# Cross-attention scores issued behind the next tile's queries, and the last two feed-forward quads on separate banks and buffers

## The chip, the cores and the metric

One core of one Trainium2 chip runs one program. The metric is the device time of one execution in microseconds (us). Its engines each work through their own list of instructions in order: TensorE (PE, matrix products and transposes into PSUM; PEld is its weight load), VectorE (DVE), ScalarE (ACT), GpSimd (POOL) and SyncE (SP), which issues the DMAs. Semaphores order them: `then_inc` on one instruction, `wait_ge` before another. An engine that waits holds up all that is behind it in its list.

## The reference

The input is `x`, 32 sequences of 64 rows of 128 features, with a context of the same shape. Eight sub-layers are applied one after the other, each to a layer-normalised `x` and added back:

```
x = x + L0_xattn(layernorm(x), ctx)   # 16 heads of 64, full softmax with a mask, own biases
x = x + L0_ffn(layernorm(x))          # 6 layers: local attention (rotary, band mask) + x, then
                                      # layernorm, W1, a * gelu(gate), W2, + x ; tokens shifted
x = x + L1_xattn(...) ; x = x + L1_ffn(...)   # 16 heads of 8 ; an fp8 product
x = x + L2_xattn(...) ; x = x + L2_ffn(...)   # mixture of 8 experts and a shared one
x = x + L3_xattn(...) ; x = x + L3_ffn(...)   # int8-rounded weights ; 8 experts
```

The change touches L0_xattn (the *cross stage*), the end of the six layers of L0_ffn (the *local stage* and its *tail*), and the rounding of L3's weights (`quantise_...`) and L1's fp8 weight, which are done on the side during the cross stage.

## The kernel before

The 2048 rows of `x` are 16 tiles of 128. `layers_tensor`, `layers_scalar`, `layers_vector` and `layers_gpsimd` (one function for each engine) run the same loop over a step number `g`, and the order of the calls in it is the order of the engine's instructions. Steps -16 to -1 start the 16 tiles of the cross stage, one each (`is_cross`). Steps 0 to 95 start the 96 tiles of the local stage (6 layers of 16; `STEPS` is 96). The loop ends at step 109 (`STEPS + OUTPUT`). Then `merged_tensor` and its fellows run L1 to L3.

A tile's work is spread over several steps. In step `g` of the cross stage TensorE does, in this order (letters are used below): the queries of tile g into PSUM `w0` (Q, `cross_queries`, L558), the values of g-1 into `w2` (V, `cross_values`, L578), the keys of g into `w1` (K, `cross_keys`, L568), the output rows of g-3 into `py` (R, `cross_rows`, L597), the transpose of the normalised x of g+1 into `pt` (X, `turn_x`, L551), the transposes of the probabilities of g-2 into `w2` (T, `turn_probs`, L692), the scores of g-1 into `w1` (S, `cross_scores`, 64 small matmuls in `scores_tensor`, L399), and the attention product of g-2 into `w2` (A, `attend_tensor`, L413). VectorE does: `cross_shift` of g-2 (adds the mask, L936, takes the maximum, L429, subtracts it, L432), layer-norm statistics of g+2, the query bias of g (L929), the normalisation of g+2 and of the finished g-4 (L466), the sums of the exponentials of g-2 (L440, L443), the update of x with R (L946), and the output bias of g-2, which copies A's result to `oT` (L956). ScalarE does the exponential of g-2 (L424), then copies V of g-1 (L880), K of g (L883), X of g+1 (`xT`, L855) and T of g-2 (`probT`, L895). GpSimd multiplies the probabilities of g-2 with the reciprocal sums (L454).

The numbers of the instructions are per tile, so `g-2` on VectorE in step g is the tile whose scores TensorE wrote in step g-1. S of g-1 waits for `kT_ready` of g, since it overwrites `w1`; T waits for `prob_ready` of g-2; A for `pT_ready`; V of g-1 for `oT_ready` of g-3; K of g for `masked` of g-2.

In the feed-forward of the local stage four tiles are a *quad*; there are 24. `quad_at(g, lag)` says which quad has its turn: quad Q is transposed into `pt` (`quad_in`, L723) in step 4Q+8, normalised in 4Q+10 (`quad_normalise`, L1022, after `quad_stats` and GpSimd's `quad_rstd`), goes through three hidden chunks (`quad_turn` L729, `affine` L838, `hidden` L741 and L745, `gelu` L844, `gate` L1030) in 4Q+11, and its output (`output`, L752) is added to the rows by `feed` (L1004 to L1007) in 4Q+13. All quads share `pt`, `py`, and the buffers `xs`, `xnT`, `gate` and `hid`. After the last quads `turn_out` (L763, L764) and `add_back` (L1038) bring the rows back to `x`, a quarter at a time, on `w0`, `w1`, `w2`, `w0`.

Of the kernel before, what the change touches and what calls it, by code (L numbers as in the profile page):

```python
# [38 lines left out]
def build(nc, a, out):  # L39
    ctx = ExitStack()  # L40
    with ctx:
# [138 lines left out]
        k.s_k8 = wide(k.straight).rearrange("p (s j n) -> p s j n", s=2, j=8)  # L180
        k.f_int, k.f_mag = (wide(k.sq)[:, i * P:(i + 1) * P].bitcast(mybir.dt.int32) for i in range(2))
# [137 lines left out]
        k.quant.spread = sem("quant_spread")  # L319
        k.quant.done = sem("quant_done")  # L320
# [166 lines left out]
NEWTON = 4  # L487

# [31 lines left out]
def quad_at(g, lag):  # L520

    Q, r = divmod(g - lag, 4)
    return Q if not r and 0 <= Q < ALL_QUADS else None
# [15 lines left out]
def layers_tensor(pe, k):  # L539
    def turn_x(g):  # L540
# [8 lines left out]
        if g - 2 == QUANTISE:  # L549
            pe.wait_ge(k.quant.done, 1)  # L550
# [164 lines left out]
    def quad_in(Q):  # L715

        pe.wait_ge(k.row_added, 2 * Q + 2)
        if Q:
            pe.wait_ge(k.gated, 3 * Q)
        else:  # L720
            pe.wait_ge(k.z_ready, QUADS)
        for j in range(4):
            mm = pe.transpose(k.pt[:, j * P:(j + 1) * P], shifted_rows(k, (4 * Q + j) % TILES), k.ident[:, :])  # L723
        mm.then_inc(k.quad_rows, 1)

    def quad_turn(Q):
        pe.wait_ge(k.quad_norm, Q + 1)
        for j in range(4):
            mm = pe.transpose(k.pt[:, j * P:(j + 1) * P], k.xs[:, 0, j, :], k.ident[:, :])  # L729
        mm.then_inc(k.quad_cols, 1)  # L730

    def hidden(Q, c, g):
        at, n = CHUNKS[c]
        if c == 0:
# [3 lines left out]
            pe.wait_ge(k.z_fed, quads_before(g, OUTPUT))  # L738
        else:
            pe.wait_ge(k.gated, 3 * Q + c)  # L740
        pe.matmul(k.pt[0:n, :], k.c_w1[:, HID + at:HID + at + n], k.xnT[:, :], start=True,  # L741
# [3 lines left out]
        pe.matmul(k.py[0:n, :], k.c_w1[:, at:at + n], k.xnT[:, :], start=True, stop=True).then_inc(k.line_psum, 1)  # L745

    def output(Q, g):
        pe.wait_ge(k.hid_ready, 3 * Q + 3)
        pe.wait_ge(k.row_added, pairs_before(g))
        for c, (at, n) in enumerate(CHUNKS):  # L750
            n += c == 2
            mm = pe.matmul(k.py[:, :], k.c_w2[0:n, c, :], k.hid[0:n, c, :], start=(c == 0), stop=(c == 2))  # L752
        mm.then_inc(k.out_psum, 1)

    def turn_out(q):

# [12 lines left out]
    for g in range(-TILES, STEPS + OUTPUT + 1):  # L769
# [16 lines left out]
        if is_cross(g - 1):  # L786
# [1418 lines left out]
```

## Time and profile before

| | us |
|---|---|
| median of 3 runs | 2528.41 |
| lowest and highest | 2522.78, 2529.38 |
| the profiled execution | 2521.92 |
| its span, first to last instruction | 2520.1 |
| mean granted TensorE clock in it | 0.984 |

The stages lie in the span about as follows: loads and start to 14.6 us, cross stage to about 254, local stage to about 1697, its tail to 1728.4, L1 to L3 to the end. All times below are microseconds from the span's start.

How to read the rows. [...] A row of the timeline has start, duration, engine, line, operation, output<-inputs, form and count, and in brackets how long the engine was idle before it and who released it. The view of one line gives shortest/median/longest duration in ns, and the first and last start in us.

### The profile page before, as it was taken

Reading aid. Unit: us, or ns where it says so; the run is one execution under the profiler, and the core shown is the slowest. Engines: PE = TensorE matmul, PEld = TensorE weight load, DVE = VectorE, ACT = ScalarE, POOL = GpSimd, SP = SyncE. Lnnn points to the kernel's source line nnn. Section 1 sums busy time; section 2 is a strip of 40 time slices with the busy share of each in tenths; the row PEclk is TensorE's granted clock in tenths of the full one; section 3 lists DMA queues with packets and bytes.
Section 4 is the critical chain, followed back from the end, with each engine's and each line's share of the span. In section 5 each row is a group of like instructions: output and inputs, shape, how many; then the busy total and the mean of one; then the engine's idle time right before and its main releaser. Section 6 shows DMA issues by size and latency. Waiting matters only on the chain.

```text
span 2520.1 us, 60784 instructions
## 1 busy us (share of the span) xinstructions
PE 2371.4 (94%) x25500; PEld 1437.9 (57%) x25500; DVE 1904.4 (76%) x3471; ACT 1453.2 (58%) x2047; POOL 1186.5 (47%) x883
## 2 busy tenths in 40 slices
PE   6787899999999999999999999988889999999999
PEld 5666556566665666666665666554555555455443
DVE  4666999999999899999999999965866766455222
ACT  2233566666666666666666666653467677566443
POOL 1222777777677767777767776741211111001000
PEclk9899999999999999999999999999899999999999
DMA  3000000000010000000000000001000101120110
GB/s 123 6 6 8 2 2 2 27 10 13 2 35 2 13 18 18 7 7 27 10 8 7 27 10 11 2 1 75 18 32 15 35 12 40 41 83 20 38 52 28
DMA packets 36164, 56.27 MB, mean 22 GB/s; under 512 B 6380, under 2 KB 20852, under 8 KB 35640
## 3 DMA queue, kind: packets, MB, share of 16 engines
q1 hardware_dynamic: 35896, 52.40, 6.7%
q8 instruction: 205, 3.36, 0.6%
q14 instruction: 63, 0.52, 0.1%
HBM read 51.19 MB, written 1.19 MB: 21 GB/s over the span
## 4 chain that ended last, share of the span: by engine, by line
PE 54%; DVE 28%; ACT 11%; issue 5%; POOL 1%; SPq 0%; DMA 0%; DVEq 0%; ACTq 0%
PE w L1380 9%; PE w L1370 9%; DVE turned L976 4%; DVE norm L983 4%; PE w L643 4%; PE w L624 4%; PE w L634 4%; PE py L658 4%; PE w L413 3%; DVE top L429 3%; DVE straight_odd L971 2%; DVE logit L432 2%; PE w L711 2%; ACT sq L877 2%; PE w L1499 2%
## 5 line engine op out<-in xcount | busy, mean ns | idle before, releaser
L424 ACT ACTIVATE prob<-logit 128x512 f32<-128x512 f32 x224 | 137.5, 630 | 299.0 <-DVE logit L432 299.0
L1370 PE MATMUL w<-qT,m_fc 128*128 128x512 f32 x544 | 267.7, 605 | 0.4 <-ACT turned L1617 0.4
L1122 POOL TENSOR_TENSOR straight_odd<-straight_odd,turned 128x1024 f32<-128x1024 f32 x96 | 227.5, 2370 | 82.5 <-DVE turned L976 79.6
L454 POOL TENSOR_TENSOR prob<-prob,rden 128x1024 f32<-128x1024 f32 x112 | 213.4, 1906 | 99.0 <-DVE rden L443 99.0
L976 DVE TENSOR_TENSOR turned<-w,rot 128x512 f32<-128x512 f32 x384 | 245.3, 680 | 0.0
L1122 POOL TENSOR_TENSOR straight<-straight,turned 128x1024 f32<-128x1024 f32 x96 | 226.6, 2370 | 37.3 <-DVE turned L976 37.3
L1116 POOL TENSOR_TENSOR straight_odd<-straight_odd,rnorms 128x1024 f32<-128x1024 f32 x96 | 180.6, 1903 | 115.3 <-DVE rnorms L997 115.3
L983 DVE TENSOR_REDUCE norm<-sq 128x16 f32<-128x1024 f32 x192 | 224.0, 1207 | 0.0
L1116 POOL TENSOR_TENSOR straight<-straight,rnorms 128x1024 f32<-128x1024 f32 x96 | 180.6, 1901 | 69.9 <-DVE rnorms L997 69.9
L643 PE MATMUL w<-b_wqkv,m_proj 128*128 128x512 f32 x384 | 191.3, 621 | 4.0 <-DVE logit L432 4.0
L890 ACT COPY qT<-w 128x1024 f32<-128x1024 f32 x96 | 97.3, 1014 | 162.0 <-PE w L670 162.0
L624 PE MATMUL w<-b_wqkv,m_proj 128*128 128x512 f32 x384 | 190.4, 618 | 0.0
L634 PE MATMUL w<-b_wqkv,m_proj 128*64 128x512 f32 x768 | 186.0, 605 | 0.0
L473 POOL TENSOR_TENSOR fresh_roots<-fresh_means,eps 128x1 f32<-128x1 f32 x64 | 12.7, 198 | 361.6 <-DVE fresh_means L461 361.6
L658 PE MATMUL py<-oT,b_wo 128*128 128x256 f32 x768 | 175.8, 382 | 1.1 <-ACT oT L911 1.1
L658 PEld LDWEIGHTS py<-oT,b_wo 128*128 128x128 f32 x768 | 147.1, 192 | 42.1 <-issue 22.8
L877 ACT ACTIVATE sq<-w 128x1024 f32<-128x1024 f32 x96 | 98.2, 1023 | 114.2 <-PE w L643 114.2
L692 PE MATMUL w<-ident,prob 128*128 128x128 f32 x896 | 122.0, 281 | 38.1 <-POOL prob L454 37.3
L895 ACT COPY probT<-w 128x1024 f32<-128x1024 f32 x112 | 114.1, 1018 | 75.9 <-PE w L692 75.9
L1617 ACT ACTIVATE turned<-w,m_bfc 128x512 f32<-128x512 f32 x136 | 93.3, 688 | 109.7 <-PE w L1370 106.8
L1617 ACT ACTIVATE straight_odd<-w,m_bfc 128x512 f32<-128x512 f32 x136 | 93.6, 688 | 105.8 <-PE w L1370 103.2
L413 PE MATMUL w<-probT,v 64*64 64x64 f32 x7168 | 134.0, 225 | 21.5 <-ACT probT L895 19.8
(253 smaller groups left out, 5255.5 us busy)
## 6 DMA issues: line engine op xcount, KB each, us to landing
b_wqkv<-gates SPq DMA_DIRECT2D x64, 256.0 KB, 3.7
b_wqkv<-in_b_wqkv SPq DMA_DIRECT2D x18, 512.0 KB, 3.6
ctxT<-in_ctxT SPq DMA_DIRECT2D x64, 64.0 KB, 1.8
b_wo<-in_b_wo SPq DMA_DIRECT2D x6, 512.0 KB, 3.6
m_fc<-in_m_fc SPq DMA_DIRECT2D x1, 2304.0 KB, 9.4
m_proj<-in_m_proj SPq DMA_DIRECT2D x1, 2304.0 KB, 13.0
m_fc<-in_m_fc SPq DMA_DIRECT2D x8, 256.0 KB, 3.5
m_proj<-in_m_proj SPq DMA_DIRECT2D x8, 256.0 KB, 3.4
```

What stands on the lines that cost most here:

```text
L413: mm = pe.matmul(w[64 * c:64 * c + 64, at:at + 64], k.v2[r, s, b, 64 * h:64 * h + 64], k.probT[r, h, 64 * b:64 * b + 64], start=True, stop ...
L454: pool.tensor_tensor(flat, flat, k.rden[:, s, :, None].broadcast_to([P, HEADS, SEQ]), ALU.mult).then_inc(k.prob_ready, 1)
L624: mm = pe.matmul(k.w0[:, 512 * c:512 * c + 512], shifted_rows(k, g % TILES), k.b_wqkv[:, 512 * c:512 * c + 512], start=True, stop=True)
L634: mm = pe.matmul(k.w2[64 * p:64 * p + 64, 512 * b:512 * b + 512], k.z[:, 2 * t + b, :], k.b_wqkv[:, 2048 + 512 * p:2560 + 512 * p], start= ...
L643: mm = pe.matmul(k.w1[:, 512 * c:512 * c + 512], shifted_rows(k, g % TILES), k.b_wqkv[:, 1024 + 512 * c:1536 + 512 * c], start=True, stop= ...
L658: mm = pe.matmul(k.py[:, 0:2 * P], k.b_wo[:, h, :], k.oT[:, h, :, :].rearrange("p a n -> p (a n)"), start=(h == 0), stop=(h == PAIRS - 1))
L976: last = dve.tensor_tensor(k.turned[:, i, :, to], heads[:, :, of], rot[:, 2 * i + 1, None, to].broadcast_to([P, HEADS, half]), ALU.mult)
L983: dve.tensor_reduce(k.norm2[:, i, :], k.sq[:, i, :, :], AX.X, ALU.add).then_inc(norm2, 1)
L1116: pool.tensor_tensor(k.straights[s][:, i, :, :], k.straights[s][:, i, :, :], k.rnorms[:, s, i, :, None].broadcast_to([P, HEADS, HD]), ALU. ...
L1122: pool.tensor_tensor(k.straights[s][:, i, :, :], k.straights[s][:, i, :, :], k.turned[:, i, :, :], ALU.add).then_inc(added, 1)
L1370: pe.matmul(claim(("hidden", J, c)), k.m_fc[:, x, c * P:(c + 1) * P], k.m_xT[:, q, :], start=True, stop=True).then_inc(k.ring_full, 1)
L1380: mm = pe.matmul(acc, k.m_proj[:, x, c, :], k.m_hid[J % 2][:, c, :], start=(c == 0), stop=(c == 3))
```

## The change

1. **Cross stage, TensorE.** S of g-1 moves from behind T to the front of the step, between Q of g and V of g-1. It no longer waits for the keys of g (which now come after it) but only for its own keys. K of g waits for `masked` of g-1 instead of g-2 (S of g-1 now uses `w1` just before it). T of g-2 moves ahead of R; X of g+1 is now behind it.
2. **Cross stage, the others.** Mask, maximum and shift of g-1 (not g-2) open VectorE's step, and the sums of g-1 follow the query bias, ahead of the two normalisations. ScalarE's exponential of g-1 stands between the copy of V and that of K. GpSimd scales g-1.
3. **Weights on the side.** `quantise_spread` moves behind the statistics; one operation of `quantise_weights` becomes `quantise_step`, early in the next step; the rest moves one step later and the fp8 weight two. TensorE's X waits for `quant.step` instead of `quant.done`; `quant.done` is waited for in L3's first queries.
4. **The last quad (23)** gets `w1` as banks (`gate_bank`, `line_bank`) and buffers of its own (`xs2`, `xnT2`, `gate2`, `hid2`, on memory that is free by then). It is transposed and normalised in step 99 (the hidden step of quad 22), has its hidden step in 100 and its output in 102 instead of 100, 102, 103 and 105. The loop ends at step 102. `turn_out` and `add_back` alternate `w0` and `w2`.

```diff
@@ buffers
+        k.xs2 = k.xs[:, 1, :, :]
+        k.xnT2 = k.kT[:, :, :, :].rearrange("p a h n -> p (a h n)")[:, 0:512]
...
+LAST_STEP = 6
+LAST_QUAD = {TURN: 3, NORMALISE: 3, HIDDEN: 4, OUTPUT: 6}
...
 def quad_at(g, lag):
+    if g == STEPS + LAST_QUAD[lag]:
+        return ALL_QUADS - 1
     Q, r = divmod(g - lag, 4)
-    return Q if not r and 0 <= Q < ALL_QUADS else None
+    return Q if not r and 0 <= Q < ALL_QUADS - 1 else None
+def line_bank(k, Q):
+    return k.w1[:, 512:1024] if Q == ALL_QUADS - 1 else k.py[:, :]
+def gate_bank(k, Q):
+    return k.w1[:, 0:512] if Q == ALL_QUADS - 1 else k.pt[:, :]
+def back_bank(k, q):
+    return (k.w0, k.w2)[q % 2]
@@ TensorE
     def cross_keys(g):
-        pe.wait_ge(k.kT_ready, T)
-        pe.wait_ge(k.masked, T - 1)
+        pe.wait_ge(k.masked, T)
...
     def cross_scores(g):
-        T = FIRST + g
-        pe.wait_ge(k.qT_ready, T + 1)
-        if is_cross(g + 1):
-            pe.wait_ge(k.kT_ready, T + 2)
-        else:
-            pe.wait_ge(k.kT_ready, T + 1)
-            pe.wait_ge(k.k_turned, T + 2)
+        pe.wait_ge(k.qT_ready, FIRST + g + 1)
+        pe.wait_ge(k.kT_ready, FIRST + g + 1)
         scores_tensor(pe, k, g % 2)
...
         if is_cross(g - 1):
+            cross_scores(g - 1)
             cross_values(g - 1)
...
+        if is_cross(g - 2):
+            turn_probs(g - 2, before)
         if is_cross(g - 3):
             cross_rows(g - 3)
...
-        if before2:
+        if before2 and not is_cross(g - 2):
             turn_probs(g - 2, before)
         if before and g >= 1:
             turn_keys(g - 1, this)
-        if is_cross(g - 1):
-            cross_scores(g - 1)
@@ ScalarE
-        if before2:
-            exp_scalar(act, k, T - 2, s, 0.125 if is_cross(g - 2) else 8.0)
+        if before2 and not is_cross(g - 2):
+            exp_scalar(act, k, T - 2, s, 8.0)
...
+        if is_cross(g - 1):
+            exp_scalar(act, k, T - 1, 1 - s, 0.125)
         if is_cross(g):
             act.wait_ge(k.k_psum, T + 1)
@@ VectorE
-        if is_cross(g - 2):
-            cross_shift(g - 2)
-        elif before2:
+        if is_cross(g - 1):
+            cross_mask(g - 1)
+            cross_shift(g - 1)
+        if before2 and not is_cross(g - 2):
...
+        if g == QUANTISE:
+            quantise_spread(dve, k)
+        if g == QUANTISE + 1:
+            quantise_step(dve, k)
         if is_cross(g):
             query_bias(g)
+        if is_cross(g - 1):
+            softmax_sum_vector(dve, k, T - 1, 1 - s)
+        elif before2 and not is_cross(g - 2):
+            softmax_sum_vector(dve, k, T - 2, s)
         if is_cross(g + 2):
             cross_normalise(g + 2)
         if is_cross(g - 4):
             cross_fresh(g - 4)
-        if before2:
-            softmax_sum_vector(dve, k, T - 2, s)
...
+        if g == STEPS + LAST_QUAD[TURN]:
+            dve.wait_ge(k.o_psum, FIRST + STEPS)
+            dve.memset(k.hid2[64:P, 2, :], 1.0)
+            quad_stats(ALL_QUADS - 1)
         if hid is not None:
             gate(hid, 0)
+        if g == STEPS + LAST_QUAD[TURN]:
+            quad_normalise(ALL_QUADS - 1)
...
-        if g == QUANTISE + 1:
+        if g == QUANTISE + 2:
             quantise_weights(dve, k)
-        if g == QUANTISE + 2:
+        if g == QUANTISE + 4:
             fp8_weight_vector(dve, k)
```

## Rows read from the trace of the kernel before

**Rows 1.** Busy times by stretch: 13 cross steps, two single steps, most of local.
```profile
43.24:237.07 193.83, 155.21 (x2520) 128.28 (x2521) 123.90 (x219) 58.21 (x83) 47.50 (x73) 0.92 0.02 6
90.59:104.64 14.05, 11.03 (x194) 8.95 (x195) 11.89 (x23) 4.32 (x6) 3.75 (x6) 1.00 0.02 6
195.22:210.41 15.19, 12.25 (x194) 10.14 (x195) 8.95 (x16) 4.32 (x6) 3.75 (x6) 0.89 0.02 5
240.00:1640.00 1400.00, 1356.51 (x17481) 851.83 (x17478) 1279.25 (x2242) 887.56 (x1165) 1007.05 (x521) 1.00 0.04 12
```

**Rows 2.** View of line L956, VectorE, from 43 to 237.5 us.
```profile
L956 DVE TENSOR_TENSOR oT<-w,a_to x14: 1223/1225/1225, 43.2 to 237.1; 128x1024 f32<-128x1024 f32 x14
```

**Rows 3.** Timeline of one cross step at full clock, 90 to 105 us.
```profile
90.44 2.05 PE L558 MATMUL w<-xT,m_fc 128*128 128x128 f32 x16
...
91.73 1.22 DVE L936 TENSOR_TENSOR logit<-w,a_mask 128x1024 f32<-128x1024 f32 x1
...
92.43 1.94 PE L578 MATMUL w<-m_fc,ctxT 128*64 128x512 f32 x8
...
94.29 2.05 PE L568 MATMUL w<-ctxT,m_fc 128*128 128x128 f32 x16
...
96.18 1.95 PE L597 MATMUL py<-m_fc,oT 128*128 128x128 f32 x16
...
97.97 0.27 PE L551 MATMUL pt<-ident,normed 128*128 128x128 f32 x1
98.28 0.27 ACT L855 COPY xT<-pt 128x128 f32<-128x128 f32 x1 [0.27 <-PE pt L551]
...
99.20 1.90 POOL L454 TENSOR_TENSOR prob<-prob,rden 128x1024 f32<-128x1024 f32 x1 [2.29 <-DVE rden L443]
...
101.25 1.06 PE L692 MATMUL w<-ident,prob 128*128 128x128 f32 x8 [3.01 <-POOL prob L454]
...
102.24 1.16 PE L399 MATMUL w<-kT,qT 64*64 64x64 f32 x64
102.35 1.01 ACT L895 COPY probT<-w 128x1024 f32<-128x1024 f32 x1 [3.81 <-PE w L692]
...
103.41 1.16 PE L413 MATMUL w<-probT,v 64*64 64x64 f32 x64
```

**Rows 4.** Timeline: TensorE's transposes after a wait, at either clock.
```profile
205.88 1.94 PE L692 MATMUL w<-ident,prob 128*128 128x128 f32 x8 [2.94 <-POOL prob L454]
...
220.34 1.06 PE L692 MATMUL w<-ident,prob 128*128 128x128 f32 x8 [2.28 <-POOL prob L454]
```

**Rows 5.** Timeline and view of line L466: VectorE beside a running GpSimd operation.
```profile
65.64 1.90 POOL L454 TENSOR_TENSOR prob<-prob,rden 128x1024 f32<-128x1024 f32 x1 [2.29 <-DVE rden L443]
66.51 1.04 DVE L1192 TENSOR_SCALAR wdiag<-ident,wmaxT 4x4 f32<-4x4 f32 x1
...
L466 DVE SCALAR_TENSOR_TENSOR y_all<-x_all,fresh_means,fresh_roots x64: 336/352/1293, 63.7 to 2342.8; 128x128 f32<-128x128 f32 x64
```

**Rows 6.** Timeline of VectorE where the cross stage meets the local stage.
```profile
244.06 1.23 DVE L971 TENSOR_TENSOR straight<-w,rot 128x1024 f32<-128x1024 f32 x1
...
253.27 1.19 DVE L956 TENSOR_TENSOR oT<-w,a_to 128x1024 f32<-128x1024 f32 x1
...
271.33 1.21 DVE L429 TENSOR_REDUCE top<-w 128x16 f32<-128x1024 f32 x1
```

**Rows 7.** Timeline of the tail, quads 22 and 23.
```profile
1697.77 0.66 PE L729 MATMUL pt<-ident,xs 128*128 128x128 f32 x4 [2.42 <-DVE xs L1022]
...
1705.22 0.75 DVE L1030 SCALAR_TENSOR_TENSOR hid<-py,c_cols,gate 85x512 f32<-85x512 f32 x1 [1.18 <-PE py L745]
...
1706.58 2.74 PE L752 MATMUL py<-hid,c_w 128*128 128x512 f32 x6
...
1710.85 1.37 DVE L1022 TENSOR_SCALAR xs<-pt,mv,rstd 128x128 f32<-128x128 f32 x4
...
1728.43 0.29 DVE L459 BATCH_NORM_STATS2 norm_stats<-x_all 128x6 f32<-128x128 f32 x1
```

More of the change, by code:

```diff
@@ L319, in build @@
         k.quant.spread = sem("quant_spread")
+        k.quant.step = sem("quant_step")
         k.quant.done = sem("quant_done")
@@ L520, in quad_at, with quad_buffers @@
 def quad_at(g, lag):
+    if g == STEPS + LAST_QUAD[lag]:
+        return ALL_QUADS - 1
     Q, r = divmod(g - lag, 4)
-    return Q if not r and 0 <= Q < ALL_QUADS else None
+    return Q if not r and 0 <= Q < ALL_QUADS - 1 else None
[3 more added lines that the diff above has]
+    return k.w1[:, 0:512] if Q == ALL_QUADS - 1 else k.pt[:, :]
+def quad_buffers(k, Q):
+    return (k.xs2, k.xnT2, k.gate2, k.hid2) if Q == ALL_QUADS - 1 else (k.xs[:, 0, :, :], k.xnT, k.gate, k.hid)
+def back_bank(k, q):
+    return (k.w0, k.w2)[q % 2]
 def pairs_before(g):
@@ L768, in layers_tensor @@
     pe.wait_ge(k.loaded, 16 * N_URGENT)
-    for g in range(-TILES, STEPS + OUTPUT + 1):
+    for g in range(-TILES, STEPS + LAST_STEP + 1):
         this, before, before2 = stages_of(g)
@@ L843, in gelu @@
         act.wait_ge(k.gate_psum, 3 * Q + c + 1)
-        act.activation(k.gate[0:n, c, :], k.pt[0:n, :], ACT.Gelu, bias=k.c_cols[0:n, 5 + c:6 + c]).then_inc(k.gated, 1)
+        act.activation(quad_buffers(k, Q)[2][0:n, c, :], gate_bank(k, Q)[0:n, :], ACT.Gelu, bias=k.c_cols[0:n, 5 + c:6 + c]).then_inc(k.gated, 1)
     def unshift(q):
@@ L858, in layers_scalar @@
     turned_x(-TILES)
-    for g in range(-TILES, STEPS + OUTPUT + 1):
+    for g in range(-TILES, STEPS + LAST_STEP + 1):
         T, s = FIRST + g, g % 2
@@ L998, in refine_norms, with feed @@
                                  op1=ALU.mult).then_inc(k.newton_step, 1)
-    def feed(first, n):
-        cols = k.py[:, 0:n * SEQ].rearrange("p (b n) -> p b n", n=SEQ)
+    def feed(bank, first, n):
+        cols = bank[:, 0:n * SEQ].rearrange("p (b n) -> p b n", n=SEQ)
         low, high = k.z[0:64, first:first + n, :], k.z[64:P, first:first + n, 1:SEQ]
@@ L1029, in gate @@
         dve.wait_ge(k.gated, 3 * Q + c + 1)
[L1030 to L1031 removed]
+        dve.scalar_tensor_tensor(out=quad_buffers(k, Q)[3][0:n, c, :], in0=line_bank(k, Q)[0:n, :], scalar=k.c_cols[0:n, 2 + c:3 + c],
+                                 in1=quad_buffers(k, Q)[2][0:n, c, :], op0=ALU.add, op1=ALU.mult).then_inc(k.hid_ready, 1)
     def add_back(q):
[L1034 removed]
+        w = back_bank(k, q)
         dve.wait_ge(k.back_psum, q + 1)
@@ L1044, in layers_vector @@
     dve.wait_ge(k.loaded, 16 * N_URGENT)
-    for g in range(-TILES, STEPS + OUTPUT + 1):
+    for g in range(-TILES, STEPS + LAST_STEP + 1):
         T, s = FIRST + g, g % 2
@@ L1080, in layers_vector @@
             dve.wait_ge(k.row_psum, p + 1)
-            feed(4 * p % (2 * TILES), 4).then_inc(k.row_added, 1)
+            feed(k.py, 4 * p % (2 * TILES), 4).then_inc(k.row_added, 1)
         if out is not None:
             dve.wait_ge(k.out_psum, out + 1)
-            feed(8 * out % (2 * TILES), 8).then_inc(k.z_fed, 1)
-        if quad_at(g, TURN) is not None:
+            feed(line_bank(k, out), 8 * out % (2 * TILES), 8).then_inc(k.z_fed, 1)
+        if quad_at(g, TURN) is not None and g < STEPS + LAST_QUAD[TURN]:
             quad_stats(quad_at(g, TURN))
-        if quad_at(g, NORMALISE) is not None:
+        if quad_at(g, NORMALISE) is not None and g < STEPS + LAST_QUAD[TURN]:
             quad_normalise(quad_at(g, NORMALISE))
@@ L1139, in layers_gpsimd @@
     pool.wait_ge(k.loaded, 16 * N_URGENT)
-    for g in range(-TILES, STEPS + OUTPUT + 1):
+    for g in range(-TILES, STEPS + LAST_STEP + 1):
         T, s = FIRST + g, g % 2
@@ L1150, in layers_gpsimd @@
             rstd_gpsimd(pool, k, k.norm, T + 2, s)
-        if before2:
+        if is_cross(g - 1):
+            softmax_scale_gpsimd(pool, k, T - 1, 1 - s)
+        elif before2 and not is_cross(g - 2):
             softmax_scale_gpsimd(pool, k, T - 2, s)
```

56 lines of the change are left out of this document (32 added, 24 removed).

## The prediction

> **What bounds the kernel now.** I read the busy times by stretch first, because the change touches the first tenth of the span and a short tail, and the share of busy time over the whole span says nothing of either. In the local stage TensorE is busy 1357 of 1400 us at full clock, in the cross stage only 155 of 194 us, at a granted clock of 0.92 [rows 1]. So there is idle time to win in the cross stage and next to none in the local stage. Then I read how often the cross stage goes round: the copy to `oT` comes 14 times, from 43.24 to 237.07 us [rows 1, 2], so a step takes 193.83 / 13 = 14.91 us. The chain of waits says why. It goes through no single engine: mask, maximum, subtraction, query bias, sums on VectorE, the multiplication on GpSimd, then T, S and A on TensorE, and `oT` on VectorE again, and the next mask follows at once because S of the next tile stood between T and A. The timeline of one step [rows 3] shows the gap: X ends at 98.24, T starts at 101.25, with GpSimd's 1.90 us as the last thing waited for. The rest of TensorE's step is dense. In the tail I read the timeline: quad 23 goes through its whole series (transpose, statistics, root, normalise, hidden, output) after quad 22's, on an almost idle chip [rows 7].
>
> **Part 1, the steady cross step.** With S of g-1 ahead of V, K and T, the probabilities of g-1 are wanted by T only in the next step. From the start of the mask to the start of GpSimd's multiplication the step shows 7.47 us [rows 3]; two normalisations of 0.35 us leave that stretch, overlapping a little, so some 6.9, and with 1.9 us on GpSimd the probabilities are there 8.9 us after S ended. T comes 16 us after it (a whole step, and V and K of the next). That chain has 7 us to spare, so what is late next is TensorE itself, or something in its order.
>
> TensorE's own work, start to start [rows 3]: Q 1.99, V 1.86, K 1.89, R 1.79, X 0.27, T 0.99, S 1.17, A about 1.1; the sum is 11.06 (busy time in such a step: 11.03 [rows 1]). But one wait is new. X now stands behind T on TensorE, and on ScalarE the copy of X (`xT`) still stands ahead of the copy of T (`probT`). A needs `probT`, so A waits for X, `xT` and `probT` one after the other. From the row of X to that of `xT` 0.04, `xT` 0.27, `probT` 1.01, 0.05 to A [rows 3]: 1.37, less the 0.1 by which two operations of one engine overlap, 1.3. Queued behind the waiting A are Q of the next tile and everything after it; nothing covers it. The step is 11.06 + 1.3 = 12.36.
>
> Is another engine later? ScalarE: exponential and both copies, 4.3 us busy [rows 1], its waits on the subtraction end before K's product is there. VectorE: `rden` ends 6.9 us after the mask started. Now the two normalisations come right behind it, beside GpSimd's multiplication, where before they came ahead of it. An operation of VectorE that meets a running GpSimd operation can be held: one on 4x4 elements, started at 66.51, took 1.04 us and ended when GpSimd's 65.64 + 1.90 was over, and the normalisation of 352 ns has taken 1293 once [rows 5]. I take the second of the two as held to 8.9, then it, the update and its statistics to 10.0, and `oT` 1.22 to 11.2. That is under 12.36 by 1.1 us, so it costs nothing in a plain step. [...]
>
> So 13 steps gain 13 x (14.91 - 12.36) = 33.2 us. From that go the things that idle time hid before: two groups of four transposes of finished rows, 0.66 each by such a group in the tail [rows 7], 1.3 together; one small product and transpose for the weights, 0.3; and the work on the weights, which stands ahead of `oT` and so ahead of V. The fp8 weight adds 11.89 - 8.95 = 2.9 us of VectorE to its step [rows 1], of which 1.1 is covered; the int8 one I take as alike: 1.5 each, 3.0 (bounds: 0, and 6 uncovered). The moved waits on the weights cost nothing while those steps have their cover.
>
> **Part 2, the start.** The first S now precedes V and K of the second tile, but the first T still waits for the first softmax and two more Qs. Laid out from the same durations, the first `oT` comes near 41.3 instead of 43.24: 1.9 gained (bounds 0 and 5, the latter all of V, K and the key copy).
>
> **Part 3, the junction.** The step-0 softmax is now tile -1's, in the step where local work starts, and ScalarE's exponential stands there behind the square of the local keys and the copy of V. From the end of A(-3): Q 1.99, transposes 0.66, S 1.17, so the mask starts at 3.8 and the subtraction ends at 7.5. V and K end near 7.6, then ScalarE squares (1.0), copies V (1.0) and only then takes the exponential, so the sums start at 10.2 and end, with `rden`, at 11.7; a normalisation, and the small rotation table held behind GpSimd's 1.9; first rotation at 13.7. Before it was at 244.06 - 237.07 = 7.0 [rows 2, 6]. So 6.7 us are lost here. Step 1 in turn has no softmax, whose parts are 1.22 + 1.22 + 1.29 + 1.3 + 0.25 = 5.3 us of VectorE. But V(0) waits for `oT`(-2), TensorE has idled some 7 us before it, and will be at half clock for V(0) and K(1), on which the rotation of the keys waits. Where that point lay 271.33 - 253.27 = 18.1 us behind `oT`(-2) before [rows 6], I get 16.9: 1.2 back. Net -5.5 (bounds 0 and -8).
>
> **Part 4, local stage.** Only a wait that has long been met is added to the keys. 0. The shift passes through unchanged, since the stage waits for its own engines and not for a clock of its own.
>
> **Part 5, the tail.** Quad 22's turn starts at 1697.77 and its last `gate` ends at 1705.97: 8.2 us [rows 7]. Quad 23's transposes slip in under `affine`, its statistics, root and normalisation (1.37 [rows 7]) between the gates; that costs quad 22 about 0.2. TensorE turns quad 23 behind `turn_out(0)` near 1706.3, so its `gate` ends near 1714.5. Output 22 goes in front of it, behind the last line product at 1713.7; two outputs of 2.74 to 1719.2; `feed` 1.5; then three `add_back` of 0.75 queue on VectorE, where before only one was left: 1723.0 instead of 1728.43. 5.4 gained (bounds: 2, if TensorE falls to half clock in between; 7).
>
> **Sum.** 33.2 - 1.3 - 0.3 - 3.0 + 1.9 - 5.5 + 5.4 = 30.4 us. Against the profiled execution, 2521.92 - 30.4 = 2491.5. That execution was 6.5 us under the median of the runs shown, and I expect the median to move by the same: 2528.41 - 30.4 = 2498.0.
>
> **Rivals.**
> *The junction costs nothing* and the weights stay hidden: 30.4 + 5.5 + 3.0 = 38.9, so 2489.5. For it: ScalarE has slack in step 1. Against: the order of ScalarE is fixed in the code. 0.15.
> *Half clock stays in the cross stage.* TensorE was slow (T 1.94 instead of 1.06) after an idle of 2.94 us and not after 2.28 [rows 4]; now it idles 1.3 per step, so I expect full clock. If every step keeps a stretch as in the row 195.22 to 210.41, it costs 15.19 - 14.05 = 1.14 x 13 = 15 us: 2513. 0.11. [...]
> *VectorE becomes the bound*: a second hold of 1.9 in each step brings its round from 11.2 to 13.1, 0.8 over TensorE's: 13 x 0.8 = 10, 2508. 0.12.
> *Slower*: TensorE is now the bound of the cross stage, so half clock there is paid in full. A step wholly at half clock costs 11.06 x (1.94 / 1.06 - 1) = 9.2 us more, 120 in 13: 2618. It turns the sign from 3.3 such steps on. Against: no stretch without a wait over 2.3 us shows it. 0.02.
> *The order changes and the loop remains*, for a wait I have overlooked ties S to the old T: 0, tail alone, 2523. 0.02.
> My forecast has 0.56, something else 0.02.
>
> **How the numbers follow.** 0.3% (7.6 us) is about what a measurement of this kernel can tell from no change. All cases but the last two and part of "something else" are beyond it: faster 0.96, same 0.02, slower 0.02. The range takes the three large cases with most of their bounds, 2484 to 2514.
>
> **What would show it.** Right: `oT` every 12.4 us with 1.3 us of idle before A, ended by `probT`; clock 1.00 in the cross stage; no idle before T; first `oT` near 41, 14th near 206; VectorE idle for 2.6 us ahead of the sums of step 0; L1's first statistics some 30 us earlier. Wrong: a step over 13 us, TensorE waiting for `oT` ahead of V (VectorE is the bound), T or S near 1.9 us (half clock), or a local stage of another length than before.

## The result, and the profile after

| | before | after |
|---|---|---|
| median, us | 2526.02 (4 runs, 2522.78 to 2529.38) | 2488.84 (4 runs, 2488.13 to 2491.89) |
| ratio, 95% interval | | 0.9855 [0.9837, 0.9873] |
| profiled execution, us | 2521.92 | 2488.49 |
| its span, mean granted clock | 2520.1, 0.984 | 2486.7, 0.991 |

The median fell by 37.2 us, the profiled execution by 33.4. The forecast was 30.4 less, 2498.0 by the median with a range of 2484 to 2514: the sign, the mechanism and the range held, and the gain is 3 us larger in the profile and 7 by the medians.

Where it lies, from the milestones that the prediction named (start in each span, us):

| | before | after | gained by then |
|---|---|---|---|
| first `oT` | 43.24 | 43.52 | -0.3 |
| 14th `oT` | 237.07 | 203.90 | 33.2 |
| first maximum of local scores | 271.33 | 243.15 | 28.2 |
| first `xs` of quad 22 | 1696.35 | 1668.02 | 28.3 |
| L1's first statistics | 1728.43 | 1695.40 | 33.0 |
| end | 2520.1 | 2486.7 | 33.4 |

So the cross loop gives 33.5, the junction takes 5.0, the local stage nothing, and the tail gives 4.7.

The busy times by stretch, kernel after: the 13 cross steps, the junction up to the first local maximum, the local stage, the tail (they answer to [rows 1]). A row has the stretch, its length, the busy time with the number of instructions for PE, PEld, DVE, ACT and POOL, then the mean granted TensorE clock, the DMA share and GB/s.
```profile
43.52:203.90 160.38, 142.36 (x2520) 117.91 (x2521) 137.66 (x219) 58.38 (x83) 47.60 (x73) 1.00 0.03 7
203.90:243.15 39.25, 26.82 (x364) 16.31 (x364) 27.81 (x44) 12.61 (x19) 18.43 (x15) 0.91 0.03 8
240.00:1640.00 1400.00, 1363.47 (x17610) 855.89 (x17600) 1276.54 (x2243) 894.19 (x1173) 1007.19 (x520) 1.00 0.04 12
1668.02:1695.40 27.38, 21.78 (x80) 9.13 (x80) 14.63 (x37) 9.77 (x17) 1.21 (x2) 0.94 0.00 1
```
The same 2520 matrix instructions take 160.38 us where they took 193.83. The granted clock there went from 0.92 to 1.00. (Full clock is a granted clock of 1.00 here, half clock one near 0.50: in the kernel before, T took 1.06 us at 220.34, at 1.00, and 1.94 at 205.88, at 0.50 [rows 4].) VectorE's busy time grew by 13.8 us with the same 219 instructions: that is not work but holding, and the rows below show where.

One plain cross step, from A to A, out of the timeline of the kernel after (answers to [rows 3]).
```profile
143.05 1.16 PE L418 MATMUL w<-probT,v 64*64 64x64 f32 x64 [1.27 <-ACT probT L922]
144.14 2.05 PE L583 MATMUL w<-xT,m_fc 128*128 128x128 f32 x16
144.96 1.19 DVE L985 TENSOR_TENSOR oT<-w,a_to 128x1024 f32<-128x1024 f32 x1
...
146.12 1.16 PE L404 MATMUL w<-kT,qT 64*64 64x64 f32 x64
147.22 1.94 PE L602 MATMUL w<-m_fc,ctxT 128*64 128x512 f32 x8
147.35 1.23 DVE L963 TENSOR_TENSOR logit<-w,a_mask 128x1024 f32<-128x1024 f32 x1 [1.20 <-PE w L404]
...
149.08 2.05 PE L592 MATMUL w<-ctxT,m_fc 128*128 128x128 f32 x16
...
150.97 1.04 PE L712 MATMUL w<-ident,prob 128*128 128x128 f32 x8
...
151.85 1.95 PE L616 MATMUL py<-m_fc,oT 128*128 128x128 f32 x16
...
153.63 0.27 PE L576 MATMUL pt<-ident,normed 128*128 128x128 f32 x1
153.94 0.27 ACT L880 COPY xT<-pt 128x128 f32<-128x128 f32 x1 [1.22 <-PE pt L576]
...
154.10 1.02 ACT L922 COPY probT<-w 128x1024 f32<-128x1024 f32 x1
...
154.31 1.90 POOL L459 TENSOR_TENSOR prob<-prob,rden 128x1024 f32<-128x1024 f32 x1 [1.77 <-DVE rden L448]
154.33 2.03 DVE L471 SCALAR_TENSOR_TENSOR y_all<-x_all,fresh_means,fresh_roots 128x128 f32<-128x128 f32 x1
155.18 1.16 PE L418 MATMUL w<-probT,v 64*64 64x64 f32 x64 [1.27 <-ACT probT L922]
```
Start to start: A 1.09, Q 1.98, S 1.10, V 1.86, K 1.89, T 0.88, R 1.78, X 0.28 and a wait of 1.27 before A; together 12.13. T no longer waits for GpSimd. The one wait left is that of A for `probT`, whose copy (154.10) stands on ScalarE behind `xT` (153.94), which waits for X (153.63). The copy of T's result could have begun when T ended, near 152.0. On VectorE `y_all` takes 2.03 us beside GpSimd's 1.90.

The waits of that stretch (engine, line, released by: us in total, times, longest), 40 to 205 us.
```profile
PE w L418 <- ACT probT L922: 17.0, 13, 1.7
...
DVE logit L963 <- PE w L404: 16.2, 11, 2.0
...
PE w L602 <- DVE oT L985: 2.8, 2, 1.7
```
VectorE waits for S in 11 instances, so it has slack; TensorE waits for `oT` ahead of V in two, the steps with the weights' work.

The junction, timeline of the kernel after (answers to [rows 6]).
```profile
211.08 1.02 ACT L902 ACTIVATE sq<-w 128x1024 f32<-128x1024 f32 x1 [3.17 <-PE w L663]
212.00 1.01 ACT L905 COPY v<-w 128x1024 f32<-128x1024 f32 x1
212.89 1.16 ACT L429 ACTIVATE prob<-logit 128x512 f32<-128x512 f32 x2
...
213.57 1.28 DVE L445 TENSOR_REDUCE den<-prob 128x8 f32<-128x512 f32 x2 [2.43 <-ACT prob L429]
...
215.21 2.19 POOL L459 TENSOR_TENSOR prob<-prob,rden 128x1024 f32<-128x1024 f32 x1 [9.76 <-DVE rden L448]
215.22 0.42 DVE L991 TENSOR_TENSOR rot<-rope,b_scales 128x256 f32<-128x256 f32 x1
...
215.68 1.22 DVE L1000 TENSOR_TENSOR straight<-w,rot 128x1024 f32<-128x1024 f32 x1
...
226.24 3.44 PE L653 MATMUL w<-b_wqkv,m_proj 128*64 128x512 f32 x8 [6.04 <-DVE oT L985]
```
The first rotation comes 11.8 us after the 14th `oT` instead of 7.0, with VectorE idle for 2.43 us behind a late exponential; and V(0) of the next step, after 6.04 us of idle TensorE, runs at half clock (3.44 us, granted clock 0.55).

The tail, timeline of the kernel after (answers to [rows 7]).
```profile
1674.84 1.36 DVE L1051 TENSOR_SCALAR xs<-w,mv,rstd 128x128 f32<-128x128 f32 x4
...
1678.94 0.66 PE L751 MATMUL w<-ident,xs 128*128 128x128 f32 x4
...
1686.37 2.74 PE L776 MATMUL py<-hid,c_w 128*128 128x512 f32 x6
...
1688.95 2.74 PE L776 MATMUL w<-v,c_w 128*128 128x512 f32 x6
...
1693.22 2.15 DVE L1067 TENSOR_TENSOR x_all<-x_all,w 128x256 f32<-128x256 f32 x6
...
1695.40 0.29 DVE L464 BATCH_NORM_STATS2 norm_stats<-x_all 128x6 f32<-128x128 f32 x1
```
Both outputs stand behind each other and three `add_back` queue behind them, as laid out.

### The profile page after: what moved, and what is told of

The parts are those of the page before. It is cut to its first block, busy times and chain, and to the rows that moved or that the text cites. A ratio compares the mean times of both kernels' runs of the same rounds, so it can differ in the third digit from the quotient of the medians.

```text
span 2486.7 us, 60786 instructions
## 1 busy us (share of the span) xinstructions
PE 2357.1 (95%) x25500; PEld 1425.8 (57%) x25500; DVE 1918.3 (77%) x3472; ACT 1452.7 (58%) x2047; POOL 1185.6 (48%) x883
## 4 chain that ended last, share of the span: by engine, by line
PE 57%; DVE 25%; ACT 12%; issue 4%; POOL 0%; SPq 0%; DMA 0%; DVEq 0%; ACTq 0%
PE w L1427 9%; PE w L1417 9%; DVE turned L1005 4%; DVE norm L1012 4%; PE w L663 4%; PE w L653 4%; PE w L643 4%; PE py L678 3%; PE w L418 3%; DVE top L434 2%; DVE straight_odd L1000 2%; ACT sq L902 2%; PE w L731 2%; PE w L1548 2%; ACT sq L893 2%
## 5 line engine op out<-in xcount | busy, mean ns | idle before, releaser
L905 ACT COPY v<-w 128x1024 f32<-128x1024 f32 x112 | 113.2, 1010 | 85.3 <-PE w L602 85.3
L418 PEld LDWEIGHTS w<-probT,v 64*64 64x64 f32 x7168 | 115.5, 135 | 76.1 <-ACT probT L922 57.5
```

Source lines behind the costliest of these rows:

```text
L418: mm = pe.matmul(w[64 * c:64 * c + 64, at:at + 64], k.v2[r, s, b, 64 * h:64 * h + 64], k.probT[r, h, 64 * b:64 * b + 64], start=True, stop ...
```

## The experiments

Eight kernels in two sets, each set compared with the kernel before on its own chip: 2525.43 us there for the first four (19 runs), 2524.56 for the last four (9 runs). The kernel after wasn't run in either set, so a difference from it goes over the kernel before, whose median moved by up to 1.5 us between the sets. The length of a stretch comes from each kernel's own profile.

**1. The tail's change alone, on the kernel before.** The two theories: the parts add, or one hides in the other.
```diff
+LAST_STEP = 6
+LAST_QUAD = {TURN: 3, NORMALISE: 3, HIDDEN: 4, OUTPUT: 6}
...
+def back_bank(k, q):
+    return (k.w0, k.w2)[q % 2]
```


> The kernel before with the change of the tail alone (quad 23 on banks and buffers of its own, loop to step 102). My theory: the two halves of the change are independent, and the tail is worth the 4.7 us that the trace of after shows between the transposes of quad 22 and the first statistics of L1 (30.7 us before, 26.0 after). Time: 4 to 6 us under before. Rival: the tail's gain was lent by the cross stage (a shifted start, another clock): 0 to 2 us under before.

2518.69 us (10 runs), ratio 0.9977 [0.9967, 0.9986]: 6.7 us less, a little over the 4 to 6 expected. Its tail takes 26.21 us from `xs` to L1's statistics.

**2. The cross stage's change alone: the kernel after with the old tail.**
```diff
-LAST_STEP = 6
+LAST_STEP = OUTPUT
...
-    return (k.w0, k.w2)[q % 2]
+    return (k.w0, k.w1, k.w2, k.w0)[q]
```


> The changed kernel with the old tail. My theory: 29 to 32 us under before, the oT copies of tiles -16 to -3 come 160 us apart as in after (194 before), and the first statistics of L1 come 30.7 us after the transposes of quad 22. Rival (the halves help each other): clearly less than the time of after plus 5.

2496.84 us (4 runs), ratio 0.9887 [0.9872, 0.9902]: 28.6 us less, just short of the 29 to 32 expected. The stretch of 13 steps is 160.38 us again, to the second decimal. The tail was expected to be as long as before and wasn't: from the transposes of quad 22 to L1's first statistics it took 34.5 us and not 30.7. 28.6 and 6.7 make 35.3, and both together gave 36.6 by the ratio: they add, within what the intervals leave open.

What the tail is worth isn't one number, though. Busy times from `xs` of quad 22 to L1's statistics: the new tail alone, the old tail behind the new cross stage, the old tail before.
```profile
1699.45:1725.66 26.21, 20.19 (x80) 8.26 (x80) 14.64 (x38) 9.77 (x17) 1.21 (x2) 1.00 0.00 1
```
```profile
1669.13:1705.03 35.90, 26.06 (x80) 10.37 (x80) 14.22 (x36) 9.67 (x17) 1.21 (x2) 0.81 0.00 1
```
```profile
1696.35:1728.43 32.08, 22.29 (x80) 8.72 (x80) 14.21 (x36) 9.68 (x17) 1.21 (x2) 0.94 0.00 1
```
The same 80 matrix instructions keep TensorE busy for 20.2, 26.1 and 22.3 us, at a granted clock of 1.00, 0.81 and 0.94. Over all the profiles the old tail took 32.1 us (before), 35.8 (experiment 4) and 35.9; the new one 26.2 (experiments 1 and 6), 27.4 (after, 3, 7 and 8) and 28.7 (experiment 5). The profile of before that the prediction rests on had caught the old tail in a short form. So the 5.4 forecast, like the 4.7 between the two profiles, lies in the lower part of what the profiles allow, 3.4 to 9.7 us; the commonest values, 35.8 and 27.4, are 8.4 apart, and the 6.7 measured by itself lies inside.

The junction has two forms too. V(0) and K(1) at this kernel's junction, and K(1) in the kernel after:
```profile
224.72 3.68 PE L650 MATMUL w<-b_wqkv,m_proj 128*64 128x512 f32 x8 [6.03 <-DVE oT L979]
228.33 3.02 PE L660 MATMUL w<-b_wqkv,m_proj 128*128 128x512 f32 x4
```
```profile
229.61 1.98 PE L663 MATMUL w<-b_wqkv,m_proj 128*128 128x512 f32 x4
```
Here the half clock lasted beyond V(0) (granted clock 0.50 in it, 0.65 in K(1)), as the prediction had said (T and R behind K took 1.54 and 3.18 us, in the kernel after 1.09 and 1.95). From the 14th `oT` to the first local maximum it is 42.15 us, 2.9 more than in the kernel after, with the same order. Experiments 3, 5 and 6 took 41.8 to 42.2 as well, so the 39.25 of the kernel after is the exception.

**3. Is A's wait real, and is it the order of two copies?** The kernel after, with the copy of T ahead of that of X on ScalarE.
```diff
         if is_cross(g + 1):
+            if before2:
+                act.wait_ge(k.pT_psum, T - 1)
+                act.copy(k.probT[:, :, :], k.w2[:, :]).then_inc(k.pT_ready, 1)
             turned_x(g + 1)
...
-        if before2:
+        if before2 and not is_cross(g + 1):
```


> The changed kernel with two copies of ScalarE exchanged in the cross steps: probT of g-2 ahead of xT of g+1. My theory: the wait of A (1.27 us in each step) is only the order of ScalarE's list; without it TensorE's round is 10.9 us, and VectorE's, with the normalisation held behind GpSimd, is about as long (10.9 from the mask to the end of oT), so a step takes about 11.0 instead of 12.13 and the kernel is 13 to 15 us faster than after. Rival 1 (VectorE is not near its limit): 16 to 17 us, with TensorE at 10.85 a step. Rival 2 (A waits for something else as well): less than 5 us.

2479.33 us (4 runs), ratio 0.9817 [0.9802, 0.9832]: 46.1 us under before, some 9 under the kernel after; 13 to 15 were expected. The wait is real and it is the order: plain steps fell from 12.13 to 10.83 us, by the 1.3, and within the 13 steps TensorE no longer waits for `probT`. But the stretch fell only from 160.38 to 150.12, by 10.3 us of the 15.2 that its 12 waits of 1.27 had taken. The waits show most of the rest.
```profile
DVE logit L966 <- PE w L404: 7.5, 7, 1.9
PE w L602 <- DVE oT L988: 6.6, 6, 2.8
```
VectorE, which had slack of 16.2 us in waits for S, has 7.5 left, and TensorE now waits for `oT` in six steps instead of two, 3.8 us more in all. Behind one of these waits it also fell to half clock for a moment (V at 115.99 took 2.65 us instead of 1.94, at a granted clock of 0.71; in the whole stretch the clock is 0.99 and the busy time 1.2 us longer). The two make up the difference. The second rival of the prediction (VectorE becomes the bound) is thus where this order leads and not where the change led.

**4. How much of the gain is clock?** The kernel before, with eight matrix products of no use between X and T, where TensorE waited for GpSimd. They fill the idle time and take nothing from the order.
```diff
+        if is_cross(g):
+            for i in range(8):
+                pe.matmul(k.w2[:, 512 * (i % 2):512 * (i % 2) + P], k.a_lx[:, 0:P], k.ident[:, :], start=True, stop=True)
         pe.wait_ge(k.prob_ready, T + 1)
```


> The kernel before with eight extra 128x128 products on TensorE in each of the 16 cross tiles, between X and T, into the bank that T overwrites: nothing is reordered, TensorE only works some 2 us of the 3 that it idled. The output is the reference's. My theory: a third of the gain of the cross stage is not the shorter chain but the clock: 8 of 13 steps before held a stretch at half clock (15.2 to 15.5 us against 14.05). With the idle filled the granted clock stays 1.00, the plain steps take 14.05, and the kernel is 8 to 11 us faster although it does more. Rival (the clock is a by-product and costs nothing here): no change, or 2 us slower for each bit of fill that overruns its cover.

2520.25 us (10 runs), ratio 0.9978 [0.9969, 0.9988]: 5.2 us less, and the expectation of 8 to 11 was missed. The eight plain steps went from 119.8 us together to 112.3, that is from as much as 15.5 each to 14.0, at a clock of 1.00 (one of them):
```profile
120.00:134.00 14.00, 13.30 (x214) 11.19 (x214) 8.95 (x16) 5.45 (x9) 3.77 (x7) 1.00 0.02 6
```
That gained 7.5. But in the two steps with the weights' work the products stood behind the wait for the weights, near half clock (0.57 over the 3.32 us below) and covered by nothing:
```profile
68.54 0.45 PE L551 MATMUL pt<-ident,normed 128*128 128x128 f32 x1 [3.01 <-DVE wdiag L1195]
68.78 3.32 PE L692 MATMUL w<-ident,m_fc 128*128 128x128 f32 x16
```
These steps grew by 1.9 and 2.1 us, and the junction, where two more tiles are filled, by 1.5 (35.79 instead of 34.26). My expectation had taken all steps for plain ones. These parts add up to some 2 us of gain; the medians say 5.2 (3.0 to 7.8 by the interval), and the rest isn't placed. The experiment still answers the question it was made for: a plain step at full clock and with the old order takes 14.0 us; with the new order 12.13. So of the 15.3 us that most steps took, about 1.3 was half clock and 1.9 the order. Both are in the 14.91 that the prediction took as the step before, so its 13 x 2.55 us is gain by order and by clock together. The fill adds 1.95 us of TensorE work (the same row in a plain step, at 131.34) and the step got shorter: that part of the loop was in truth waiting, and its price was the clock.

**5. Is VectorE held at the cost of the step?** The kernel after, with `y_all` ahead of the sums, so that it isn't beside GpSimd's multiplication.
```diff
+        if is_cross(g - 4):
+            cross_fresh(g - 4)
         if is_cross(g - 1):
             softmax_sum_vector(dve, k, T - 1, 1 - s)
...
-        if is_cross(g - 4):
-            cross_fresh(g - 4)
```


> The kernel after, with the normalisation of the tile before (y_all) moved on VectorE from behind the sums of the scores to ahead of them, so that it no longer runs beside GpSimd's scaling. Theory: in a plain step VectorE has slack, and the hold (y_all 2.03 us at 142.20 where 0.7 to 1.0 is its length alone) ends before anything waits for it; so the plain steps keep their 12.13 us, and only the two steps with weight work (14.57 and 14.99 us, in which V waits 2.8 us for oT in two instances) give back up to 1.3 us each: 0 to 3 us in all, plain steps within 0.2 of 12.13. It could also cost: the sums start some 1 us later, and so do GpSimd's scaling and T. Rival, the hold is on the path of each step: 13 steps by about 1.2 us, 15 us, and oT(-16) to oT(-3) falls from 160.4 to about 145. Second rival, the sums are what T waits for: 13 steps lose about 0.9 us each, 172 us for the stretch.

2489.12 us (4 runs), ratio 0.9851 [0.9836, 0.9866]: no difference from the kernel after (0.9855). The plain steps kept 12.12 us, the stretch lost 1.75 (158.63), within the 0 to 3 expected. VectorE's busy time in it fell from 137.66 to 123.44 us by this one move. The hold is real and covered, as the prediction took it. The expectation put the length of `y_all` alone at 0.7 to 1.0 us; its row in experiment 6 says 0.34.

**6. Both orders.** Copy of T first, and `y_all` ahead of the sums.
```diff
...
+            if before2:
+                act.wait_ge(k.pT_psum, T - 1)
+                act.copy(k.probT[:, :, :], k.w2[:, :]).then_inc(k.pT_ready, 1)
             turned_x(g + 1)
...
+            cross_fresh(g - 4)
         if is_cross(g - 1):
             softmax_sum_vector(dve, k, T - 1, 1 - s)
```


> The kernel with the copy of the turned probabilities ahead of the copy of the turned tile on ScalarE (copy order: 10.83 us a plain step, stretch 150.12 us), and with the normalisation of the tile before ahead of the sums on VectorE as well. Theory: with the wait for probabilities gone, TensorE and VectorE are nearly level (V waits 0.35 us for oT in a plain step, more in the steps with weight work, 6.6 us in six instances), so taking the 1.2 us hold out of VectorE's order brings the stretch from 150.1 to 144 to 147 us; plain steps 10.5 to 10.8, the steps with weight work 13.6 to about 12. Rival, the two levels are reached by TensorE alone: within 1 us of the copy order by itself. Second rival, the scaling then starts later and T becomes the last to wait: plain steps 11.3 to 11.8, 158 us for the stretch.

2474.11 us (5 runs), ratio 0.979 [0.9777, 0.9804]: 5 to 7 under experiment 3 (by medians and by ratios), 50 under before. The stretch is 145.33 us, within the 144 to 147 expected, plain steps 10.8. The steps with the weights' work didn't shrink to 12 as expected (13.97 and 14.47 us); those right behind them did, from 10.86 to 9.2. Busy times of that stretch, and the row of `y_all` with the multiplication that follows the sums:
```profile
41.98:187.31 145.33, 141.65 (x2520) 118.03 (x2521) 122.61 (x219) 58.39 (x83) 47.45 (x73) 1.00 0.03 8
```
```profile
130.63 0.34 DVE L471 SCALAR_TENSOR_TENSOR y_all<-x_all,fresh_means,fresh_roots 128x128 f32<-128x128 f32 x1
...
132.53 1.90 POOL L459 TENSOR_TENSOR prob<-prob,rden 128x1024 f32<-128x1024 f32 x1 [2.03 <-DVE rden L448]
132.54 0.28 DVE L978 TENSOR_TENSOR x_all<-x_all,py 128x128 f32<-128x128 f32 x1
```
`y_all` is back at 0.34 us, and VectorE's busy time for the same 219 instructions is 122.61 instead of 137.66: 15 us of it were holding. TensorE is busy for 141.65 of 145.33 us at a clock of 1.00. With the order right, that stage has 4 us left to gain without less work. The same edit (`y_all` early) took 1.75 us from the stretch in experiment 5, too little to show in the median, and 4.8 here. In a plain step it still takes next to nothing (10.83 to 10.79 us): the 4.8 come from the other steps.

**7. The junction: is it the exponential's place?** The kernel after, with step 0's exponential ahead of the squaring of the keys.
```diff
+        if g == 0:
+            exp_scalar(act, k, T - 1, 1 - s, 0.125)
         if this and not is_cross(g):
             act.wait_ge(k.k_psum, T + 1)
...
-        if is_cross(g - 1):
-            exp_scalar(act, k, T - 1, 1 - s, 0.125)
         if is_cross(g):
+            if is_cross(g - 1):
+                exp_scalar(act, k, T - 1, 1 - s, 0.125)
```


> The kernel after, with the exponential of step 0 (the last cross tile) ahead of the squaring of the keys on ScalarE. At the junction the exponential ran at 212.89 behind a squaring at 211.08 and the copy of the values at 212.00, and the sum behind it waited 2.43 us for it. Theory: the first rotation (215.68, 11.8 us behind oT(-3)) comes about 1.8 us earlier, and of that the end gains 1 to 2 us. Rival, V(0) of the following step waits for oT at half clock (6.04 us of waiting at 226.24), and the earlier rotation is only waited out there: less than 0.5 us of the end.

2486.84 us (4 runs), ratio 0.9845 [0.9829, 0.9861]: 0.5 to 2.5 us under the kernel after (the first by each kernel's distance from its own before, the last by the ratios), which the intervals can't tell from nothing. In the junction itself the rows can.
```profile
210.38 1.23 ACT L429 ACTIVATE prob<-logit 128x512 f32<-128x512 f32 x2 [2.66 <-DVE logit L437]
211.04 1.29 DVE L445 TENSOR_REDUCE den<-prob 128x8 f32<-128x512 f32 x2
...
213.16 1.22 DVE L1002 TENSOR_TENSOR straight<-w,rot 128x1024 f32<-128x1024 f32 x1
...
214.54 3.17 PE L616 MATMUL py<-m_fc,oT 128*128 128x128 f32 x16
...
223.72 1.94 PE L653 MATMUL w<-b_wqkv,m_proj 128*64 128x512 f32 x8 [2.65 <-DVE oT L987]
```
The sums no longer wait; the first rotation comes 9.45 us after the 14th `oT` instead of 11.78. And V(0) follows an idle time of 2.65 us instead of 6.04 and runs at full clock, 1.94 us instead of 3.44; the step behind it takes 15.63 us instead of 17.14 (and instead of 20.0 to 20.1 in experiments 2, 3, 5 and 6, which have the junction's order of the kernel after). From the 14th `oT` to the first local maximum it is 35.41 us, 3.8 less than in the kernel after and 1.1 more than before. L1's first statistics come at 1691.46 instead of 1695.40, so these 3.8 us reach the end of the tail. The rival said that the earlier rotation would only be waited out; for the stretches up to there it fell, and more came back than the 1.8 us of the theory, since V(0) kept full clock. For the end, which both spoke of, nothing is shown: from L1 on this profile took 1.6 us more than that of the kernel after.

**8. All three orders.**
```diff
+        if g == 0:
+            exp_scalar(act, k, T - 1, 1 - s, 0.125)
...
+            if before2:
+                act.wait_ge(k.pT_psum, T - 1)
+                act.copy(k.probT[:, :, :], k.w2[:, :]).then_inc(k.pT_ready, 1)
             turned_x(g + 1)
...
+            cross_fresh(g - 4)
         if is_cross(g - 1):
             softmax_sum_vector(dve, k, T - 1, 1 - s)
```


> All three orders together: copy of the turned probabilities first, normalisation of the tile before ahead of the sums, exponential of step 0 ahead of the squaring of the keys. Theory: the gains add, since they lie in different stretches: 9.5 us from the copy order (measured against the kernel after), 3 to 6 from the normalisation with it, 1 to 2 at the junction, so 13 to 17 us under the kernel after, 2472 to 2476 us. Rival, the last gain is swallowed by the half clock at the junction (the step there 20.06 us with the copy order where the kernel after has 17.14): 2477 to 2480 us.

2473.76 us (5 runs), ratio 0.9793 [0.9778, 0.9808]: the same as experiment 6. The time lies within the 2472 to 2476 expected, but experiment 6 had reached it without the third order, so that the gains add isn't shown. The junction took 35.22 us against 41.81 there, 6.6 less. Of that, in the two profiles, 1.7 went in one longer cross step, 1.2 in the tail (27.4 us against 26.2) and 2.6 behind it, where nothing was changed; the spans differ by 1.5. The longer step is one instruction, V, at half clock behind the same wait (granted clock 1.00 and 0.52). Experiment 6 and this one:
```profile
90.70 1.94 PE L602 MATMUL w<-m_fc,ctxT 128*64 128x512 f32 x8 [2.07 <-DVE oT L988]
```
```profile
90.87 3.55 PE L602 MATMUL w<-m_fc,ctxT 128*64 128x512 f32 x8 [2.07 <-DVE oT L990]
```
 Busy times of the first 100 us from L1's first statistics on, in the same order:
```profile
1680.86:1780.86 100.00, 87.17 (x819) 52.36 (x823) 80.83 (x170) 44.62 (x92) 23.15 (x61) 0.93 0.16 58
```
```profile
1676.79:1776.79 100.00, 88.16 (x803) 52.70 (x803) 78.87 (x166) 42.83 (x90) 23.08 (x61) 0.90 0.16 58
```
From there to the end experiment 6 took 788.5 us and this one 791.1. The gain of the junction's order thus can't be confirmed on top of the two others by these runs. Either version is 13 to 16 us better than the kernel after and 50 or a little more better than before.

## Why the prediction was right, step by step

**The plain step: right.** 12.36 was forecast, 12.13 measured. The wait of A for X, `xT` and `probT` was forecast at 1.3 and is 1.27, in 12 of the 13 steps. The rest of the sum, 11.06, was 10.86, because T and S were taken from rows in another order: T takes 0.88 ahead of R, not the 0.99 ahead of S, and S 1.10 ahead of V, not 1.17. So the start-to-start time of T and of S differed with the group behind them. 0.23 x 13 = 3.0 us of the surplus.

**What no idle time hides: nearly right.** The weights were put at 3.0; TensorE's waits for `oT` are 2.8, and the two pairs of steps around them exceed twice 12.13 by 1.2 and 1.6. The transposes and the small product were put at 1.6 and are 2.1: what the remaining steps have over 12.13.

**The last two steps: left out.** 11.44 and 10.69 us, 2.1 less than two plain ones. In the last there is no X of a next cross tile, so A follows R and the wait goes (1.4); in the one before, `oT` follows A at once, since `y_all` is no longer beside GpSimd's multiplication (0.7). I had multiplied one step by 13 where the last are other steps.
These four together: 13 x 12.13 + 2.8 + 2.1 - 2.1 = 160.4, the stretch measured (160.38), as it must be, since they were read from it. Forecast 165.3 by the same terms.

**The start: right in size.** From the first Q to the first `oT` 27.05 us instead of 28.64, 1.6 gained against 1.9. It doesn't show in the end, since the first Q itself, which waits for a DMA (that of `a_to`, 6.52 us instead of 4.64), came at 16.47 instead of 14.60. In the other profiles that first Q lay between 14.5 and 16.7, so this is spread of the loads and not the change.

**The junction: right in sum, by two errors.** -5.5 forecast, -5.0 measured. Step 0: -6.7 forecast, -4.8 measured. The exponential stood where it was expected, the sums started 9.7 us after the 14th `oT` (10.2 forecast), but the small rotation table wasn't held behind GpSimd's multiplication: 0.42 us, not 1.9. Step 1: +1.2 forecast, -0.2 measured: from `oT`(-2) to the first maximum 18.25 us, not 16.9. There V(0) is at half clock (3.44 us), as forecast; the size was wrong. Experiment 7, with V(0) at full clock, took 16.74 for the same stretch: my 16.9 was the figure for full clock, in a sentence that spoke of half.
There is luck in the sum as well. K(1), which the forecast also had at half clock, ran at full clock in this profile (1.98 us) and at half in that of experiment 2 (3.02 us). The four other profiles with this order lost 7.6 to 7.9 us at the junction and not 5.0, at the edge of the bound of 8.

**The local stage: right.** 1405.7 us from first to last maximum, 1405.9 before.

**The tail: right in mechanism, its worth uncertain.** 5.4 forecast, 4.7 between the profiles, 6.7 alone. The new tail's own length was well laid out: 26.7 us forecast (1723.0 - 1696.35), 26.2 to 28.7 measured. The old one it was taken from was a short one. The bound "2, if TensorE falls to half clock" named the right cause with the wrong side: the half clock is dearer in the old tail (up to 35.9 us at a granted clock of 0.81, against 28.7 at 0.88 for the new one, and 26.2 at 1.00), so it makes the change worth more.

**The median.** I let it move by as much as the profile, from a median 6.5 us above the profiled execution. The runs since put the median of before at 2524.6 to 2526.0, so 2528.41 of three runs was high, and 2526.0 - 30.4 would have been 2495.6. Of the rest, 7 us by the medians, 3.0 are the plain step and 2.1 the last two steps. The remaining 2 lie within the spread of the tail, the junction and the stages behind, and the medians can't place them. In the profiles the cross stage gave 4.9 us more than forecast, the start 2.2 less, the junction 0.5 more and the tail 0.7 less; half a microsecond lies elsewhere.

**The rivals.** Half clock in every step fell (1.00 in the stretch, no T or S near 1.9). The expectation of full clock was right, but one reason given for it wasn't: the prediction set waits of 2.28 us (full clock) against 2.94 (half) from two rows, but [rows 3] has T at full clock after 3.01. What the runs show is that 12 waits of 1.27 us, with the transposes T and X ahead of each, cost no clock: 1.00 over the stretch. VectorE as the bound fell for this change: it waits for S in 11 steps. The sign named for it, TensorE waiting for `oT` ahead of V, came in two steps, those of the weights, whose price was in the sum. It is the next in line, by experiment 3. That the loop remains fell: T never waits for GpSimd.

## What to carry to other kernels

When a wait is taken out of a loop, look at what the moved instruction now stands behind on each other engine: here one copy behind another on ScalarE cost 1.3 us a step, found on paper and worth 9 us when swapped. An order on a second engine can be worth next to nothing while the first engine still waits (experiment 5) and more once it doesn't (experiment 6: 4.8 us of the 15 that VectorE was held), so try such orders together. A part whose length depends on the clock has to be read from several profiles: the old tail and the junction each had forms 3 to 4 us apart. Multiply a step only by the number of steps that are alike, and lay out the first, the last and the odd ones by themselves.

## What the runs showed of the hardware

**Who is held when two engines start together.** `y_all` at 154.33, 20 ns after GpSimd's multiplication (154.31, 1.90), took 2.03 us where it takes 0.34 by itself. The table `rot` at 215.22, 10 ns after the same kind of multiplication (215.21), took 0.42 (0.36 is the median of its six instances), and GpSimd took 2.19 instead of 1.90. The same again in experiment 7 (`rot` 0.42, 2.19). So the start times in the records don't say who will be held; which of the two records is lengthened does. Why the one lost and the other won stays open: in both cases a normalisation (0.26 us) that had started 160 ns before GpSimd was still running. An operation with one operand in PSUM (`x_all` at 132.54 in experiment 6, 10 ns after GpSimd at 132.53) took 0.28, as at 156.28 in the kernel after, where the multiplication had ended, and GpSimd took 1.90: neither was held.

**A busy engine that does nothing.** VectorE was "busy" for 137.66 us in 219 instructions and for 122.61 in the same 219 once `y_all` stood elsewhere. An engine at 86% by that count had 15 us of holding in it.

**The clock after an idle time.** How long TensorE waited doesn't settle whether it comes back at half clock. The plainest pair is V behind a wait of 2.07 us in experiments 6 and 8: 1.94 us in one (granted clock 1.00), 3.55 in the other (0.52). In the kernel before T took 1.94 us (0.50) after waits of 2.31, 2.82 and 2.94 us, and 1.06 or 1.07 (1.00) after 2.38, 2.56, 3.01 and 3.35. In experiment 3 V took 1.94 (1.00) after 2.79 and 2.65 (0.71) after 2.43. A fall can also come with the second group and not the first: after 2.76 us T took 1.09 and R behind it 3.17 (experiment 7, 0.58) and 3.31 (experiment 8, 0.55) against 1.95. The 12 waits of 1.27 us all stayed at full clock, and each V(0) after 6.0 us (the kernel after, experiments 2, 3, 5 and 6) was at half: 3.44 and 3.68 in the two rows above, 3.68 in the others.

**Spread that isn't the change's.** From L1's first statistics to the end all ten kernels do the same, and took 788.4 to 792.9 us: 788.4 and 788.5 where the granted clock in the first 100 us was 0.93, 789.9 to 792.9 where it was 0.90. The two at 0.93 (experiments 1 and 6) are also the two whose tail ran at full clock throughout (26.2 us, 1.00). The old tail took 32.1 to 35.9 us, the new one 26.2 to 28.7, and the step behind the junction 17.1 or 20.1 in the same order. So a whole span can differ by more than the smaller effects here; experiment 7's effect is seen in its own stretch and not in its median.
